# A table of steps for each batch's projections, and rope's products in another PSUM bank, in a decoder layer on one core

## The chip, the cores and the metric

The kernel runs on one core of a Trainium2 chip. Its time is device microseconds of one execution; several executions are timed, and their median is compared. One further execution is recorded by the hardware profiler, and the rows shown here come from it.

## What is computed

A decoder layer on x of shape (4, 512, 128): four batches (0 to 3) of 512 rows. Cut to what matters:

```python
x = x + attn(layernorm(x))      # 16 heads of 8; causal
    q = xn @ W_q                                    # (512, 128)
    lat = layernorm(xn @ W_dkv) * gamma + beta      # (512, 32)
    k, v = lat @ W_uk, lat @ W_uv                   # (512, 128) each
    q, k = rope(q), rope(k)
    softmax(q k^T / sqrt(8), causal) v, then @ W_o
x = x + cross_attn(layernorm(x), ctx)   # 8 heads of 64, 32 context rows
x = x + fp4_ffn(layernorm(x))           # blockwise FP4 of activations and weights, silu(gate) * up
```

Rope on one side (0 is q, 1 is k): the product times cos, plus the product with its halves exchanged times sin.

## The kernel before

**Slots and steps.** The attention of a batch is cut into four groups of four heads. One group is one slot, so batch b fills slots 4b to 4b+3, sixteen slots in all (0 to 15), and every slot has ten steps (0 to 9). Each engine walks the same loop over slots n and steps u, and at each step it issues what the tables and the functions of the kernel give it for that step. The order on each engine is therefore written out by hand; engines meet only by semaphores.

**What a slot does.** TensorE multiplies q and k of the next group for its row maxima (`max_pair`, L1081, into three banks `mxp`, two units to a pair), and VectorE adds the mask and reduces them (`max_unit`, L832, 12 units to a slot). `PAIR_STEPS` and `MAX_STEPS` say at which step: pairs stand at steps 0, 2, 3, 4 and, for the group after, at 7 and 8. At step 6 VectorE writes the maxima as bfloat16 (L842, L844), at step 7 TensorE turns them (`max_rows`, L1090), ScalarE copies them (`nrows`), and SyncE places them with a DMA into `qs`. TensorE's `score_unit` (L1105) at steps 0, 1, 3, 5, 6, 8 feeds ScalarE's exponentials (L633, `exp_unit`), GpSimd masks them (L446) and TensorE multiplies them by the values (L1116). From slot 5 on the rows behind attention go through stages a to d of ten steps each, one tile of 128 rows entering per slot: output projection, cross-attention, FP4 feed-forward. Slots 5, 6 and 7 have one, two and three of them, later ones four. They use the banks `misc[0]` (stages a and b) and `misc[1]` (stages c and d).

**Projections ahead.** While batch b is in attention, batch b+1 is projected (`project`, called as `project(b + 1, g, u)` with g the slot within the batch). One table, `WHEN`, gives each part (slot in the batch, step): layer norm's statistics, `xn`, its transpose `xnT` (L995), the latent product `lat` (L1001), its norm `latn` (L748) and transpose `latT` (L1008, L573), and for each side the product (`cos0`, `cos1`, L1015, 128x512 in float32), the multiplication by cos on VectorE (L779, under the same entry), ScalarE's two copies of 64 rows that exchange halves (`swap`, L543), the multiplication by sin on VectorE (`sin`, L786), then on GpSimd and ScalarE the sum (L286) and its split in three bfloat16 parts (`high`, `rest` L292, `mid`, `low` L298). SyncE stores the parts in DRAM (L344) and loads them in stacked form into `qs` and `ks` (L359); the first max pairs of a batch wait for that at step 7 of the slot 4b+2 that goes before it. `values_in` (L1022) makes the batch's v at slot 4b+1, step 0, from `latT`.

Rope's products stand in `banks[MX_BANK]`, the first of the three `mxp` banks. TensorE's `claim` makes whoever writes a bank wait for the last reader of what it held, so the max pair that follows in this bank waits for the swap.

`set_up` (parts 8 to 10, L1059 and L1063) transposes the feed-forward weights in slot 1. SyncE's own loop is a fixed order of stores, loads and places per slot; at slot 4b+1 it places the maxima of slot 4b+2, then stores and loads the next batch's parts.

Of the kernel before, what the change touches and what calls it, by code (L numbers as in the profile page):

```python
# [84 lines left out]
def decoder_layer(nc, x, ctx_768, L0_attn_W_q, L0_attn_W_dkv, L0_attn_W_uk, L0_attn_W_uv, L0_attn_W_o,  # L85
# [8 lines left out]
    with ctx:  # L94
# [322 lines left out]
        def _(pool):  # L417
# [110 lines left out]
            for n in range(NSLOT + 5):  # L528
                b, g_ = n // NG, n % NG
                for u in range(10):  # L530
# [10 lines left out]
        def _(act):  # L541
# [19 lines left out]
            def project(b, g, u):  # L561
                if (g, u) == WHEN["xnT"]:
                    act.wait_ge(s["xnT_mm"], b + 1)
                    copy(xnT[:, :], misc[0][:, :]).then_inc(s["xnT_d"], 1)
# [710 lines left out]
```

## Time and profile before

| | |
|---|---|
| median of 3 runs | 421.15 us (420.87 to 424.14) |
| profiled execution, its own time | 423.29 us |
| its span, first to last instruction | 421.6 us |
| mean granted TensorE clock | 0.784 |
| TensorE busy | 298.0 us, 71% |
| VectorE busy | 299.5 us, 71% |
| ScalarE busy | 177.5 us, 42% |
| GpSimd busy | 192.8 us, 46% |

The profiled execution lies 2.1 us over the median. The first exponential of slot n marks where the slot begins. These marks stand at 47.5 us for slot 0, 99.6 for slot 3, 111.8 for slot 4, 166.2 for slot 7, 182.2 for slot 8, 249.4 for slot 11 and 320.9 for slot 15. Before 47.5 us lie the loads, batch 0's projections and the set-up of weights; behind slot 15 the rows of the last batch are finished.

### The profile page before, as it was taken

How to read it: one execution, taken by the hardware profiler on the slowest of the kernel's cores; microseconds unless marked ns; L12 is line 12 of the kernel's file. 1: busy time of each engine (PE TensorE's matmuls, PEld its weight loads, DVE VectorE, ACT ScalarE, POOL GpSimd, SP SyncE). 2: the span in 40 equal slices, each digit the busy share in tenths (PEclk: the TensorE clock that was granted, in tenths of full speed). 3: DMA queues.
4: the chain of work that ended last, by engine and by line, in shares of the span. 5: the costliest groups of instructions: out<-in, count | busy, mean ns of one | idle time of the engine just before them, and what ended most of it. 6: DMA issues, size and time to landing. Idle time of an engine off the chain costs nothing.

```text
span 421.6 us, 6515 instructions
## 1 busy us (share of the span) xinstructions
PE 298.0 (71%) x1790; PEld 144.2 (34%) x1790; DVE 299.5 (71%) x1137; ACT 177.5 (42%) x327; POOL 192.8 (46%) x374
## 2 busy tenths in 40 slices
PE   1684678757877768868785979787797664848553
PEld 1272332212234123334432434334243323536332
DVE  5467656446647576898879787899977536677882
ACT  5351355543546354445454435355545412322111
POOL 4214207322306363363757553545545535563653
PEclk9998555756768686889888588899979968665696
DMA  8069000260300052004002600040000000000000
GB/s 214 27 198 178 1 0 4 75 151 0 78 0 1 24 174 32 1 0 83 2 8 75 158 1 8 2 83 7 3 6 3 7 0 8 7 0 9 1 12 19
DMA packets 20835, 17.50 MB, mean 42 GB/s; under 512 B 1920, under 2 KB 20224, under 8 KB 20800
## 3 DMA queue, kind: packets, MB, share of 16 engines
q1 hardware_dynamic: 20272, 16.50, 16.0%
q10 hardware_dynamic: 528, 0.59, 0.5%
q8 instruction: 15, 0.25, 0.3%
q14 instruction: 20, 0.16, 0.1%
HBM read 9.62 MB, written 7.34 MB: 40 GB/s over the span
## 4 chain that ended last, share of the span: by engine, by line
PE 39%; DVE 30%; issue 11%; POOL 8%; DMA 6%; ACT 4%; SPq 1%; DVEq 0%; POOLq 0%; ACTq 0%
PE pvp L1116 9%; DVE summed L832 8%; PE mxp L1081 5%; PE st L1105 4%; DMA ks<-parts_dram 3%; PE mxp L1015 3%; PE misc L1195 3%; PE misc L1180 2%; DMA parts_dram<-parts 2%; DVE space L768 2%; POOL space L476 2%; DVE stats L737 2%; PE misc L1177 2%; DVE space L748 2%; DVE space L765 2%
## 5 line engine op out<-in xcount | busy, mean ns | idle before, releaser
L832 DVE CUSTOM_DVE_ANT_0 summed<-mxp,causal 128x512 bf16<-128x512 f32 (+3 forms) x256 | 114.0, 486 | 19.8 <-PE mxp L1081 19.3
L633 ACT ACTIVATE probs<-st 128x1024 f32<-128x1024 f32 (+1 forms) x96 | 84.6, 881 | 85.4 <-PE st L1105 85.1
L1081 PE MATMUL mxp<-ks,qs 48*128 48x512 bf16 (+3 forms) x256 | 40.8, 357 | 49.1 <-DVE rmax L832 37.9
L1116 PE MATMUL pvp<-probs,va 128*32 128x128 f32 (+3 forms) x512 | 60.4, 558 | 5.1 <-POOL probs L446 5.1
L446 POOL TENSOR_SCALAR_AFFINE_SELECT probs<-probs 128x256 f32<-128x256 f32 x128 | 48.0, 411 | 23.0 <-ACT probs L633 23.0
L543 ACT ACTIVATE space<-misc 128x128 f32<-128x128 f32 (+3 forms) x78 | 24.2, 327 | 48.5 <-PE misc L1136 18.2
L1105 PE MATMUL st<-qs,ks 50*128 50x512 bf16 (+3 forms) x256 | 41.4, 363 | 3.5 <-ACT probs L633 2.2
L1081 PEld LDWEIGHTS mxp<-ks,qs 48*128 48x128 bf16 x256 | 11.9, 98 | 69.4 <-DVE rmax L832 42.5
L476 POOL TENSOR_TENSOR space<-space 128x128 f32<-128x128 f32 (+2 forms) x33 | 24.8, 752 | 23.6 <-DVE space L771 23.6
L463 POOL TENSOR_TENSOR space<-space,xrden 128x256 f32<-128x256 f32 x16 | 9.8, 615 | 40.9 <-DVE xrden L889 40.9
L488 POOL TENSOR_TENSOR space<-space,reciph 128x352 f32<-128x352 f32 x16 | 12.6, 785 | 32.3 <-DVE reciph L759 32.3
L1105 PEld LDWEIGHTS st<-qs,ks 50*128 50x128 bf16 x256 | 10.9, 101 | 45.2 <-issue 27.3
L439 POOL TENSOR_TENSOR rstd<-var,halfneg 128x1 f32<-128x1 f32 (+1 forms) x36 | 23.0, 640 | 3.0
L437 POOL TENSOR_SCALAR var<-mv 128x1 f32<-128x1 f32 (+1 forms) x36 | 9.1, 253 | 27.7 <-DVE mv L741 26.0
L832 DVE DVE_READ_ACCUMULATOR2_ANT rmax<- 128x1 f32 x256 | 21.3, 83 | 0.0
L1116 PEld LDWEIGHTS pvp<-probs,va 128*32 128x32 f32 x512 | 11.8, 121 | 26.8 <-issue 18.5
L765 DVE TENSOR_SCALAR space<-space 128x128 int32<-128x128 int32 (+2 forms) x33 | 12.2, 369 | 9.1 <-POOL space L470 4.5
L1195 PE MATMUL misc<-wdT,space 128*128 128x128 f32 (+1 forms) x72 | 15.8, 377 | 2.3 <-ACT space L543 2.3
L779 DVE TENSOR_TENSOR turned<-mxp,cos 128x512 f32<-128x512 f32 x8 | 5.5, 692 | 16.1 <-PE mxp L1015 16.1
L1195 PEld LDWEIGHTS misc<-wdT,space 128*128 128x128 f32 (+1 forms) x72 | 13.5, 273 | 9.0 <-ACT space L543 7.6
L771 DVE SCALAR_TENSOR_TENSOR space<-space 128x128 f32<-128x128 f32 (+2 forms) x33 | 15.4, 465 | 1.1
L437 POOL TENSOR_SCALAR varl<-mvl 128x4 f32<-128x4 f32 x4 | 0.9, 230 | 29.5 <-DVE mvl L741 29.5
(196 smaller groups left out, 593.9 us busy)
## 6 DMA issues: line engine op xcount, KB each, us to landing
parts_dram<-parts SPq DMA_DIRECT2D x8, 384.0 KB, 2.6
qs<-parts_dram SPq DMA_DIRECT2D x16, 192.0 KB, 3.8
ks<-parts_dram SPq DMA_DIRECT2D x16, 192.0 KB, 4.4
parts_dram<-parts SPq DMA_DIRECT2D x8, 256.0 KB, 2.9
xin<-in_x SPq DMA_DIRECT2D x4, 256.0 KB, 8.2
parts_dram<-parts SPq DMA_DIRECT2D x8, 128.0 KB, 2.9
out<-outr SPq DMA_DIRECT2D x16, 64.0 KB, 1.6
qs<-nrows SPq DMA_DIRECT2D x32, 4.0 KB
```

The source lines that it names most:

```text
L439: g.tensor_tensor(rstd[:, sl], var[:, sl], halfneg[:, sl], ALU.pow).then_inc(s["rstd" + name], 1)
L446: last = g.affine_select(out=m, in_=m, compare_op=ALU.is_ge, fill=0.0, base=0, pattern=[[0, 2], [1, P]], channel_multiplier=-1)
L476: g.tensor_tensor(norm, norm, expo, ALU.subtract).then_inc(s[round_name], 1)
L543: return nc.scalar.activation(dst, src, ACT.Copy, scale=scale)
L633: nc.scalar.activation(probs[n % 2][:, 2 * pair:2 * pair + 2, 512 * k:512 * k + w], st2[:, :].rearrange("p (h q) -> p h q", h=2)[:, :, 0:w ...
L765: v.tensor_scalar(expo.bitcast(i32), norm.bitcast(i32), 0x7F800000, None, ALU.bitwise_and)\
L771: v.scalar_tensor_tensor(norm, norm, BIT_DOWN, expo, ALU.mult, ALU.add).then_inc(s[sum_name], 1)
L832: last = v.tensor_tensor_reduce(out=summed[:, m % 2, e * w:(e + 1) * w], in0=mxp[m % 3][:, e * w:(e + 1) * w], in1=causal[:, S - w:S], sca ...
L1081: last = mm(units[r][:, e * w:(e + 1) * w], qs[rows, c, i * P:(i + 1) * P], ks[rows, c, 0:w], start=True, stop=True)
L1105: last = mm(stp[r][:, at:at + S - P * j], ks[rows, c, j * P:(j + 1) * P], qs[rows, c, j * P:S], start=True, stop=True)
L1116: last = mm(pvp[32 * i:32 * i + 32, j * P:S], va[:, j, GH * (n % NG) + i, :], probs[n % 2][:, i, OFF[j]:OFF[j] + S - P * j], start=(j == 0 ...
L1195: last = mm(m[:, 0:DM], dqhT[0:w, k % R, c * P:(c + 1) * P], wdT[0:w, c, :], start=(c == 0), stop=(c == 2))
```

## The change

`WHEN` becomes a table for each batch (batch 0 shares batch 1's). The entry `turn` is new: VectorE's multiplication by cos gets a step of its own behind TensorE's product, where before both had the step `cos`. `swap` and `sin` follow it. In all batches the latent's statistics and norm come earlier. Batches 2 and 3 have entries with slot -1: their projections begin in the last slot of the batch before the previous one, that is at slots 3 and 7 in place of 4 and 8. The last entry, `low1`, moves from slot 4b+2 step 0 (b the batch that is in attention: slots 2, 6, 10) to slot 1 step 8 for batch 1, slot 4 step 7 for batch 2 and slot 9 step 5 for batch 3. The products go to `ROPE_BANK = 1`, which is `misc[1]`. `latT` becomes a pair of buffers, since batch 2's is written before batch 1's values are made. The three parts of `set_up` move from slot 1 to slot 2. SyncE's order is untouched.

```diff
+ROPE_BANK = 1
...
-WHEN = {"stats": (0, 0), "rstd": (0, 0), "xn": (0, 2), "xnT": (0, 3), "lat": (0, 4), "lat_stats": (0, 8),
...
-        "cos0": (0, 5), "swap0": (0, 6), "sin0": (0, 7), "cos1": (1, 5), "swap1": (1, 6), "sin1": (1, 7),
...
+           "cos0": (0, 5), "turn0": (0, 7), "swap0": (0, 8), "sin0": (0, 9), "sum0": (1, 0), "high0": (1, 1),
...
-SET_UP = [(1, 1), (1, 4), (1, 8)]
+SET_UP = [(2, 1), (2, 4), (2, 8)]
...
-        latT = sb("latT", [P, S])
+        latT = sb("latT", [P, 2, S])
...
-                    if b < B - 1:
-                        project(b + 1, g_, u)
+                    for ahead in range(1, B):
+                        project(ahead, n - NG * (ahead - 1), u)
...
-                    wait(act, "v_mm", b)
-                    nc.scalar.activation(latT[0:LAT, :], misc[0][0:LAT, :], ACT.Identity, bias=beta[:, :],
+                    wait(act, "v_mm", b - 1)
+                    wait(act, "rope_mm", 2 * b - 2)
+                    nc.scalar.activation(latT[0:LAT, b % 2, :], misc[0][0:LAT, :], ACT.Identity, bias=beta[:, :],
...
-                v.tensor_tensor(turned[:, side, 0, :], banks[MX_BANK][:, :], cos[:, :], ALU.mult)\
+                v.tensor_tensor(turned[:, side, 0, :], banks[ROPE_BANK][:, :], cos[:, :], ALU.mult)\
...
-                    if (g, u) == WHEN[f"cos{side}"]:
+                    if (g, u) == WHEN[b][f"turn{side}"]:
                         turn_cos(b, side)
...
-                    if (g, u) == WHEN[f"cos{side}"]:
-                        m = claim(MX_BANK, "swapped_d", 2 * b + side + 1)
+                    if (g, u) == WHEN[b][f"cos{side}"]:
+                        m = claim(ROPE_BANK, "swapped_d", 2 * b + side + 1)
```

The changed kernel's lines stand 16 or 17 further down, so L779 becomes L796, L786 L803, L832 L849, L1015 L1032, L1081 L1098, L1090 L1107 and L1105 L1122.

VectorE in slot 0, batch 1's first rope side, before (L779 is the multiplication by cos; ISA rows are max units, of which those of 128 columns are the last before the maxima are written):

```order
88 L832 ISA rmax 128x1
89 L779 TENSOR_TENSOR turned<-mxp,cos 128x512
90 L832 ISA summed,rmax<-mxp,causal 128x128
91 L832 ISA rmax 128x1
92 L832 ISA summed,rmax<-mxp,causal 128x128
```

and now, from the writing of the maxima at step 6 on:

```order
97 L859 CAST nparts<-rmax 128x8x2
98 L861 TENSOR_TENSOR nparts<-rmax,nparts 128x8x2
99 L754 BN_STATS statsl<-lat 128x6 x4
100 L758 BN_AGGR mvl<-statsl 128x2 x4
101 L796 TENSOR_TENSOR turned<-misc,cos 128x512
102 L849 ISA summed,rmax<-mxp,causal 128x512
103 L849 ISA rmax 128x1
104 L765 TENSOR_SCALAR latn<-lat,mvl,rstdl 128x32 x4
105 L849 ISA summed,rmax<-mxp,causal 128x512
106 L849 ISA rmax 128x1
107 L803 TENSOR_TENSOR turned<-turned,sin 128x512
```

The multiplication by cos has moved from ahead of the last max units and of the maxima's writing to behind both, and the latent's statistics and norm have come into slot 0.

TensorE at the same place, steps 5 to 8, before:

```order
28 L1105 MATMUL st<-qs,ks 128x512 x2
29 L1015 MATMUL mxp<-xnT,wq 128x512
30 L1105 MATMUL st<-qs,ks 128x384 x2
31 L1105 MATMUL st<-qs,ks 128x128 x2
32 L1090 MATMUL mxp<-identb,nparts 8x128 x4
33 L1081 MATMUL mxp<-ks,qs 128x512 x2
34 L1105 MATMUL st<-qs,ks 128x256 x2
35 L1081 MATMUL mxp<-ks,qs 128x512 x2
36 L1105 MATMUL st<-qs,ks 128x512 x2
```

and now:

```order
28 L1122 MATMUL st<-qs,ks 128x512 x2
29 L1032 MATMUL misc<-xnT,wq 128x512
30 L1122 MATMUL st<-qs,ks 128x384 x2
31 L1122 MATMUL st<-qs,ks 128x128 x2
32 L1107 MATMUL mxp<-identb,nparts 8x128 x4
33 L1098 MATMUL mxp<-ks,qs 128x512 x2
34 L1122 MATMUL st<-qs,ks 128x256 x2
35 L1098 MATMUL mxp<-ks,qs 128x512 x2
36 L1025 MATMUL misc<-ident,latn 32x128 x4
37 L1122 MATMUL st<-qs,ks 128x512 x2
```

The product L1015 keeps its place and changes its bank from `mxp` to `misc`. The transpose of the latent (L1025) now stands in slot 0, after two max pairs.

TensorE with batch 3's first side, before (slot 8, steps 5 to 7, with stages a to d around it):

```order
228 L1015 MATMUL mxp<-xnT,wq 128x512
229 L1116 MATMUL pvp<-probs,va 32x512 x4
230 L1105 MATMUL st<-qs,ks 128x384 x2
231 L1105 MATMUL st<-qs,ks 128x128 x2
232 L1180 MATMUL misc<-wguT,space 128x352
233 L1090 MATMUL mxp<-identb,nparts 8x128 x4
234 L1164 MATMUL misc<-vwo,space 128x128 x2
235 L1081 MATMUL mxp<-ks,qs 128x512 x2
```

and now (slot 7, steps 6 and 7):

```order
199 L1197 MATMUL misc<-wguT,space 128x352
200 L1107 MATMUL mxp<-identb,nparts 8x128 x4
201 L1181 MATMUL misc<-vwo,space 128x128 x2
202 L1032 MATMUL misc<-xnT,wq 128x512
203 L1098 MATMUL mxp<-ks,qs 128x512 x2
204 L1133 MATMUL pvp<-probs,va 32x384 x4
```

The product has moved from two steps ahead of the next max pair (L1081) to right in front of it, behind the up product (L1197) that uses the same bank `misc[1]`.

## Rows read from the trace of the kernel before

**Rows 1.** The page's busy times: us, share of the span, instructions.

```profile
PE 298.0 (71%) x1790; PEld 144.2 (34%) x1790; DVE 299.5 (71%) x1137; ACT 177.5 (42%) x327; POOL 192.8 (46%) x374
```

**Rows 2.** Busy time by stretch: slots 0-2, 3, 4-6, 7, 8-10, 12, 13.

```profile
core 0: us, PE busy (x) PEld busy (x) DVE busy (x) ACT busy (x) POOL busy (x), PEclk, DMA share, GB/s
47.50:99.60 52.10, 37.48 (x207) 12.61 (x207) 30.08 (x136) 25.92 (x39) 18.41 (x34) 0.57 0.18 47
99.60:111.80 12.20, 9.87 (x74) 2.88 (x72) 7.86 (x38) 6.26 (x10) 2.41 (x7) 0.71 0.04 10
111.80:166.20 54.40, 41.64 (x262) 15.56 (x260) 35.67 (x156) 27.01 (x44) 23.11 (x46) 0.75 0.23 57
166.20:182.20 16.00, 12.67 (x87) 5.24 (x87) 13.33 (x54) 8.07 (x15) 6.64 (x15) 0.89 0.01 2
182.20:249.40 67.20, 52.84 (x322) 25.65 (x322) 56.37 (x218) 32.31 (x62) 38.19 (x71) 0.82 0.21 51
268.20:286.30 18.10, 14.32 (x100) 7.03 (x101) 16.05 (x64) 8.52 (x17) 9.26 (x20) 0.91 0.25 49
286.30:303.60 17.30, 13.38 (x106) 6.53 (x105) 16.21 (x64) 8.96 (x18) 9.26 (x20) 1.00 0.02 6
```

**Rows 3.** Groups by line: busy us, mean ns | idle before them, what ended it.

```profile
L1081 PE MATMUL mxp<-ks,qs 48*128 48x512 bf16 (+3 forms) x256 | 40.8, 357 | 49.1 <-DVE rmax L832 37.9 <-ACT turned L543 7.6 <-DMA ks<-parts_dram 3.6
L779 DVE TENSOR_TENSOR turned<-mxp,cos 128x512 f32<-128x512 f32 x8 | 5.5, 692 | 16.1 <-PE mxp L1015 16.1
L786 DVE TENSOR_TENSOR turned<-turned,sin 128x512 f32<-128x512 f32 x8 | 5.5, 683 | 9.1 <-ACT turned L543 9.1
L768 DVE TENSOR_SCALAR space<-space 128x128 f32<-128x128 f32 (+2 forms) x33 | 11.8, 358 | 1.1
```

**Rows 4.** Timeline of slot 0: start us, us; in brackets idle before, and releaser.

```profile
56.11 2.08 PE L1015 MATMUL mxp<-xnT,wq 128*128 128x512 f32 x2
58.23 0.69 DVE L779 TENSOR_TENSOR turned<-mxp,cos 128x512 f32<-128x512 f32 x1 [3.42 <-PE mxp L1015]
60.23 0.59 PE L1090 MATMUL mxp<-identb,nparts 128*8 128x128 bf16 x4 [1.50 <-DVE nparts L844]
61.04 0.69 DVE L786 TENSOR_TENSOR turned<-turned,sin 128x512 f32<-128x512 f32 x1 [0.87 <-ACT turned L543]
61.27 0.61 PE L1081 MATMUL mxp<-ks,qs 48*128 48x512 bf16 x2 [0.45 <-ACT turned L543]
```

**Rows 5.** Timeline of slots 1 and 2.

```profile
78.43 0.39 PE L1081 MATMUL mxp<-ks,qs 48*128 48x512 bf16 x2 [2.02 <-ACT turned L543]
...
85.00 1.16 POOL L298 TENSOR_TENSOR parts<-turned,parts 128x512 bf16<-128x512 f32 x1 [0.39 <-ACT parts L543]
...
90.27 0.79 SPq L359 DMA_DIRECT2D ks<-parts_dram  x2
...
94.76 0.61 PE L1081 MATMUL mxp<-ks,qs 48*128 48x512 bf16 x2 [2.90 <-DMA ks<-parts_dram]
```

**Rows 6.** Timeline of slots 4 and 5.

```profile
125.70 0.39 PE L1081 MATMUL mxp<-ks,qs 48*128 48x512 bf16 x2 [2.02 <-ACT turned L543]
...
137.79 2.07 PE L1015 MATMUL mxp<-latT,wuk 128*128 128x512 f32 x2 [1.21 <-DVE rmax L832]
...
144.01 0.41 PE L1081 MATMUL mxp<-ks,qs 48*128 48x512 bf16 x2 [1.72 <-ACT turned L543]
```

**Rows 7.** Timeline of slots 8 to 10.

```profile
194.68 1.02 PE L1015 MATMUL mxp<-xnT,wq 128*128 128x512 f32 x2
...
198.11 1.19 ACT L543 ACTIVATE turned<-mxp 64x512 f32<-64x512 f32 x2
...
224.87 1.29 POOL L286 TENSOR_TENSOR turned<-turned 128x512 f32<-128x512 f32 x1
...
225.07 1.29 DVE L768 TENSOR_SCALAR space<-space 128x352 f32<-128x352 f32 x1
...
229.59 1.14 DVE L765 TENSOR_SCALAR space<-space 128x128 int32<-128x128 int32 x1
```

More of the change, by code:

```diff
@@ L431, in _ @@
                             pattern=[[-1, P]], channel_multiplier=1)
-            g.memset(latT[:, :], 0.0).then_inc(s["consts_ready"], 1)
+            g.memset(latT[:, :, :], 0.0).then_inc(s["consts_ready"], 1)
             def rstd_of(mv, var, rstd, name, sl, n):
@@ L699, in _ @@
             for name in ("xnT", "lat", "swap0", "latT", "high0", "swap1", "mid0"):
-                project(0, *WHEN[name])
+                project(0, *WHEN[0][name])
             set_up(0)
             for name in ("high1", "mid1"):
-                project(0, *WHEN[name])
+                project(0, *WHEN[0][name])
             act.wait_ge(s["cross_ready"], 1)
@@ L719, in _ @@
                         stages[stage](k, step)
-                    if b < B - 1:
-                        project(b + 1, g, u)
+                    for ahead in range(1, B):
+                        project(ahead, n - NG * (ahead - 1), u)
                     if 0 < b < B and (g, u) == VALUES_IN:
@@ L802, in project @@
                 for side in range(2):
-                    if (g, u) == WHEN[f"cos{side}"]:
+                    if (g, u) == WHEN[b][f"turn{side}"]:
                         turn_cos(b, side)
-                    if (g, u) == WHEN[f"sin{side}"]:
+                    if (g, u) == WHEN[b][f"sin{side}"]:
                         turn_sin(b, side)
@@ L943, in _ @@
             sorted_weights()
-            for name in ("lat_stats", "cos0", "latn", "sin0"):
-                project(0, *WHEN[name])
+            for name in ("lat_stats", "turn0", "latn", "sin0"):
+                project(0, *WHEN[0][name])
             rope_sum(dve, v, 0, 0)
-            project(0, *WHEN["cos1"])
+            project(0, *WHEN[0]["turn1"])
             part_rest(dve, v, 0, 0)
-            project(0, *WHEN["sin1"])
+            project(0, *WHEN[0]["sin1"])
             rope_sum(dve, v, 0, 1)
@@ L969, in _ @@
                         stages[stage](k, step)
-                    if b < B - 1:
-                        project(b + 1, g, u)
+                    for ahead in range(1, B):
+                        project(ahead, n - NG * (ahead - 1), u)
                     for ahead, m in MAX_STEPS[u]:
@@ L1003, in project @@
                     last.then_inc(s["lat_mm"], 1)
-                if (g, u) == WHEN["latT"]:
+                if (g, u) == WHEN[b]["latT"]:
                     pe.wait_ge(s["latn_d"], b + 1)
@@ L1021, in values_in @@
                 for t in range(NT):
-                    last = mm(m[:, t * P:(t + 1) * P], latT[:, t * P:(t + 1) * P], wuv[:, :], start=True, stop=True)
+                    last = mm(m[:, t * P:(t + 1) * P], latT[:, b % 2, t * P:(t + 1) * P], wuv[:, :], start=True, stop=True)
                 last.then_inc(s["v_mm"], 1)
@@ L1223, in _ @@
                         stages[stage](k, step)
-                    if b < B - 1:
-                        project(b + 1, g, u)
+                    for ahead in range(1, B):
+                        project(ahead, n - NG * (ahead - 1), u)
                     if 0 < b < B and (g, u) == VALUES_IN:
```

73 lines of the change are left out of this document (40 added, 33 removed), and 13 rows, old and new, of the table WHEN.

## The prediction, made before the changed kernel had run

> **What bounds the kernel now.** I read the busy times first: TensorE and VectorE share the lead at 71% each, so neither is full over the whole span [rows 1]. Then the busy times by stretch, since 71% is a mean over stretches with different limits [rows 2]. The reader is to see three things there. In slots 12 and 13, with four row stages and no projection, VectorE is busy 16.05 of 18.1 us and 16.21 of 17.3 us: VectorE is the bound there, with 1.1 to 2.05 us idle per slot. In slot 3, with neither rows nor projection, a slot takes 12.2 us, and TensorE (9.87 us busy at a granted clock of 0.71) is nearer to its limit than VectorE (7.86 us). And slots with a projection are longer by more than its work: slots 8 to 10 take 67.2 us against 3 x 18.1 = 54.3 us for three of slot 12, an excess of 12.9 us, while VectorE's busy time is up by 56.37 - 3 x 16.05 = 8.2 us only. Slots 0 to 2 take 52.1 us with TensorE busy 37.48, slots 4 to 6 take 54.4 with 41.64: 14.6 and 12.8 us in which TensorE stands. So I looked for what it waits for.
>
> The groups name it [rows 3]: 49.1 us of idle time ahead of the max pairs, of which 37.9 is VectorE still reducing (the ordinary pace of a ring of three banks), but 7.6 is ScalarE's swap, which holds the first `mxp` bank, and 3.6 is the load of `ks`. VectorE stands 16.1 us ahead of its eight multiplications by cos and 9.1 us ahead of the eight by sin. The timelines show how these chain. In slot 0 TensorE's rope product runs 2.08 us at half clock, VectorE waits 3.42 us for it with max units queued behind the multiplication, so the maxima are late and TensorE waits 1.50 us for them, then 0.45 us for the swap [rows 4].
>
> **The change part by part.**
>
> *Batch 1 (slots 0 to 2).* With `turn` two steps behind the product, VectorE reduces its last units and writes the maxima while TensorE multiplies; with the other bank the next max pair doesn't wait for the swap. What leaves TensorE's path: 1.50 + 0.45 us in slot 0 [rows 4] and 2.02 us in slot 1 [rows 5], together 3.97 us. The product itself (about 2 us each) stays on TensorE and stays on its path. The load: the last part is made at 85.00 + 1.16 us, the `ks` load is issued at 90.27, and the first max pair of batch 1 waits for it 2.90 us until 94.76 [rows 5]. Now `low1` comes at slot 1 step 8 in place of slot 2 step 0, two steps earlier; but slot 1 holds more of that lead, since the set-up and the latent's norm have left it. Two steps of a 16 us slot are 3.2 us, just over the 2.90 us, and the set-up now in slot 2 pushes the pair back further. The wait goes. Sum so far 6.9 us. What comes back is VectorE's wait for the swap at the step `sin`, which follows `swap` by one step. The nearest row is the 0.87 us of slot 0, where VectorE had come straight from the maxima [rows 4]; twice that is 1.7 us. Bounds: nothing comes back (6.9), or both swaps are waited for in full, 1.19 us each [rows 7], and the load still holds a half (6.9 - 2.4 - 1.45 = 3.1). I take 6.9 - 1.7 = **5.2 us**.
>
> *Batch 2 (slots 3 to 6).* The first side and the latent move into slot 3, the shortest. The waits that leave TensorE: 2.02 and 1.72 us for the swap, and 1.21 us in which the product waited for the `mxp` bank to be read [rows 6], together 4.95 us. The moved work costs the same wherever TensorE is the limit, so I count nothing for a fuller slot 3. Back come two waits at `sin`, 1.7 us. Bounds 4.95 and 4.95 - 2.4 = 2.6 us; I take **3.2 us**.
>
> *Batch 3 (slots 7 to 10).* Here VectorE is the bound, and the question is its idle time and its lengthened operations. Slots 8 to 10 have 67.2 - 56.37 = 10.8 us idle, against 3 x 2.05 = 6.2 us at slot 12's rate and 3.3 us at slot 13's [rows 2]: excess 4.6 to 7.5 us. Two operations also ran long beside GpSimd's rope work: L768 took 1.29 us, started 0.20 us into the 1.29 us sum L286, and an L765 took 1.14 us; the L768 group has a mean of 0.36 [rows 3, 7]. These are about 0.9 and 0.8 us, 1.7 in all. Rope's GpSimd work moves from steps 8, 9 and 0, where the rounding of FP4 stands on VectorE, to steps 1, 3 and 5 of slots 8 and 9. So 6.3 us could go (up to 9.2). Against it: both products now stand at step 7, right in front of the max pair that VectorE wants next. A product costs 1.02 us at full clock [rows 7] and 2.08 at half [rows 4]; two are 2.0 to 4.2 us, of which before VectorE showed 1.27 as idle only on one. I put 2.1 there. The bank is shared with stages c and d: the product must wait for `hid`, which VectorE issues a step earlier with two TensorE operations between, and stage d's transposes at step 1 wait for the swap of step 9. Half a swap each, 2 x 0.6 = 1.2 us. I take 6.3 - 2.1 - 1.2 = **3.0 us**, bounds 9.2 and -0.3 (6.3 less 4.2 and 2.4).
>
> *Edits at nothing.* The zeroing of `latT` doubles, far ahead of slot 0, beside VectorE's first statistics, for which GpSimd and TensorE wait there anyway. In the prologue the first set-up transpose uses the rope bank and now waits for the swap, but the work behind it waits for batch 0's load in any case. ScalarE's added wait for `rope_mm` names a product two batches old. SyncE's order is the same: it stores batch 2's and 3's parts only after the maxima of slots 6 and 10 are placed, so parts that are ready earlier gain nothing more than the end of the load wait. If the cover in the prologue were gone it would cost half a swap, 0.6 us.
>
> **Sum.** 5.2 + 3.2 + 3.0 = 11.4 us. The profiled execution took 423.3 us by its own time (span 421.6), so it would take 411.9; the median of the runs is 421.15, from which I predict **409.8 us**, 2.7% less. Slots 11 to 15 and the end behind them shift as they are: every slot hangs on the one before through both engines.
>
> **A rule of the Trainium skill on GpSimd's moved work.** The two long operations ran beside GpSimd instructions that read the same memory [rows 7]. The page "SBUF — State Buffer", section "Who interferes with whom", says that VectorE in its two-port modes, or with two SBUF inputs against a reading GpSimd instruction, shares a port pair under an exclusive lock, so that the second to issue blocks for the first's whole length. The trace agrees as far as it goes: VectorE's operation ended with GpSimd's.
>
> **The rivals.**
>
> *The waits only change their name.* TensorE still has two products of 2 us per batch at half clock, in slots where its clock is granted at 0.57 to 0.75 of full [rows 2]. If the max pairs come as late as now, VectorE's waits go from L779 to L832, and what goes is the load's 2.90 us. Against: the 1.50 and 2.02 us are TensorE's own waits, not VectorE's. Time 421.15 - 2.9 = 418.3. Chance 0.14.
>
> *GpSimd's sums hold VectorE six times.* Batch 3's three operations of each side last 1.16 to 1.29 us, and two of six met a VectorE operation that could be held. In the new places next to the multiplication by sin and the norms, all six could, at 0.9 us: 5.4 us in place of 1.7. Then batch 3 gives 3.0 - 3.7 = -0.7 us and the time is 413.5. This is what the lock of that page would do at worst. For it speaks that the multiplication by sin reads two SBUF tensors; against it, that steps 1 to 5 hold mostly reads of PSUM. Chance 0.12.
>
> *Slower: bank 1 and step 7 in the VectorE-bound slots.* Each product at step 7 holds back the max pair by 2.08 us, and each swap at step 9 holds back stage d's transposes, and with them the down product and the bank for stage c, by 1.19 us: 2 x (2.08 + 1.19) = 6.5 us. In batches 1 and 2 the gains then shrink to the load's 2.9 us. Time 421.15 + 6.5 - 2.9 = 424.8. It decides once these handovers cost more than the other batches gain. For it: slots 7 and 8 are the ones without slack. Against: the clock is granted at 0.82 to 0.89 there, so a product is nearer 1.02 us. Chance 0.07.
>
> *More than counted.* TensorE's granted clock is 0.57 in slots 0 to 2, where it stands most, and 1.00 in slot 13, where it hardly does [rows 2]. With fewer waits more of the matmuls run at 2.4 GHz. Taking the upper bounds, 6.9 + 4.95 + 9.2 = 21 us, gives 400; half way between that and the forecast is 405. Chance 0.15 for 401 to 405.
>
> The forecast itself, 405 to 415, has 0.52.
>
> **How the numbers follow.** A measurement of this kernel tells about 1%, or 4.2 us, from no change. Below 416.9 us lie the forecast, the better case and the six holds: 0.79, less some of their edges, 0.78. Within 1%: the renamed waits and a part of the slower rival, 0.16. Over 425.4: 0.06. The range from 402 to 418 leaves out most of the slower rival, half of the renamed waits and the edge of the best case, 2 in 10.
>
> **What would show each step.** In slots 0, 1, 4 and 5, L796 (cos) is preceded by little idle time, under 1 us, and no L1098 waits for ScalarE's swap. Slot 2 loses the wait of L1098 for the `ks` load. L803 (sin) waits 0.5 to 1.2 us. Slots 0 to 2 together take some 47 us, slots 3 to 6 some 63.5, slots 7 to 10 some 80 (83.2 now). No rounding operation (L782, L785) lasts over 1 us beside GpSimd's rope sums. I am wrong if TensorE's waits for `rmax` in slots 7 to 9 grow by what VectorE's waits for L1032 lose, or if the second set-up and latent work simply move the stall from slot 1 to slot 0.

## The result, and the profile after

The changed kernel takes 407.72 us (median of 4 runs, 405.24 to 410.85), the kernel before 422.13 us beside it (4 runs, 420.87 to 424.14). The recorded ratio is 0.972, with a 95% interval of 0.966 to 0.978; the ratio of the two medians is 0.966, at the lower end of it. The forecast was 409.8 us, a ratio of 0.973, so 11.4 us less where the medians show 14.4. Later runs of the same kernel had a median of 404.82 us. The profiled execution took 405.5 us by its own time, span 403.8 us, at a granted clock of 0.804 in place of 0.784. It lies 2.2 us under its median, and the one of the kernel before lies over its own and counts among that kernel's slower runs, so the 17.8 us between the two spans overstate the gain.

Lines have moved by 16 or 17: cos is L796, sin L803, `max_unit` L849, the product L1032, `max_pair` L1098, `max_rows` L1107, the value product L1133, the swap and ScalarE's other copies L559. The busy times of the changed kernel's page, and three of its groups by line:

```profile
PE 288.0 (71%) x1790; PEld 140.9 (35%) x1790; DVE 299.5 (74%) x1137; ACT 176.8 (44%) x327; POOL 193.7 (48%) x374
...
L849 DVE CUSTOM_DVE_ANT_0 summed<-mxp,causal 128x512 bf16<-128x512 f32 (+3 forms) x256 | 113.9, 486 | 23.6 <-PE mxp L1098 23.2
...
L1098 PE MATMUL mxp<-ks,qs 48*128 48x512 bf16 (+3 forms) x256 | 40.0, 349 | 45.1 <-DVE rmax L849 40.9 <-DMA ks<-parts_dram 3.9
L1133 PE MATMUL pvp<-probs,va 128*32 128x128 f32 (+3 forms) x512 | 55.2, 512 | 5.1 <-POOL probs L462 5.1
```

VectorE's busy time has not moved (299.5 us before and after). TensorE's has: the same 1790 matmuls took 298.0 us [rows 1] and take 288.0. So the span's 17.8 us are 10.0 us of shorter matmuls and 7.8 us less idle time (123.6 to 115.8). Of the 10.0 us, 6.2 lie in slots 0 to 10; 3.8 lie ahead of slot 0 and from slot 11 on, where the matmuls are the same in number (155 and 687) and the lengths differ by under 2 us. The value product, which the change does not touch, shows it; its line of before:

```profile
L1116 PE MATMUL pvp<-probs,va 128*32 128x128 f32 (+3 forms) x512 | 60.4, 558 | 5.1 <-POOL probs L446 5.1
```

Its 512 matmuls took 60.4 us, 558 ns each, and now take 55.2 us, 512 ns each. Of the swap's 7.6 us ahead of the max pairs [rows 3] nothing is left; the load of `ks` still holds them 3.9 us, of which 2.15 lie ahead of slot 0 (0.55 there before).

Busy times by stretch: slots 0-2, 3, 4-6, 7, 8-10, 12 and 13, against [rows 2]:

```profile
47.60:92.70 45.10, 35.19 (x207) 12.12 (x207) 31.52 (x143) 25.56 (x38) 18.92 (x34) 0.62 0.21 54
92.70:109.30 16.60, 14.61 (x88) 5.96 (x88) 11.59 (x53) 8.93 (x14) 5.07 (x9) 0.69 0.03 10
109.30:150.40 41.10, 31.12 (x242) 12.02 (x242) 29.69 (x132) 24.39 (x39) 19.64 (x41) 0.88 0.29 75
150.40:174.70 24.30, 19.04 (x103) 8.61 (x103) 18.40 (x80) 10.17 (x20) 11.22 (x23) 0.70 0.00 1
174.70:233.30 58.60, 48.33 (x308) 23.10 (x308) 52.13 (x195) 29.57 (x57) 34.38 (x65) 0.80 0.23 59
251.70:270.50 18.80, 15.08 (x100) 7.51 (x101) 16.24 (x64) 8.44 (x17) 9.26 (x20) 0.82 0.22 47
270.50:287.80 17.30, 13.38 (x106) 6.54 (x105) 16.21 (x64) 9.07 (x18) 9.25 (x20) 1.00 0.02 6
```

Slots 0 to 2 went from 52.1 to 45.1 us, slots 3 to 6 from 66.6 to 57.7, slots 7 to 10 only from 83.2 to 82.9. Slots 12 and 13, without a projection, are as they were but for 0.7 us in slot 12, at a clock of 0.82 in place of 0.91; from slot 11 on the kernel is 1.8 us shorter. In slots 3 to 6 TensorE's busy time went from 9.87 + 41.64 = 51.5 us to 14.61 + 31.12 = 45.7 us, its idle time only from 15.1 to 12.0.

Slots 7 to 10 in one stretch, before and now:

```profile
166.20:249.40 83.20, 65.51 (x409) 30.90 (x409) 69.70 (x271) 40.39 (x76) 44.83 (x86) 0.84 0.17 42
150.40:233.30 82.90, 67.37 (x411) 31.70 (x411) 70.53 (x274) 39.74 (x75) 45.60 (x88) 0.77 0.16 42
```

VectorE's idle time fell from 13.5 to 12.4 us (in slot 7 it rose from 2.7 to 5.9, in slots 8 to 10 it fell from 10.8 to 6.5), and its busy time rose from 69.7 to 70.5.

The timeline of slots 0 to 2 of the changed kernel, against [rows 4, 5]:

```profile
56.22 2.08 PE L1032 MATMUL misc<-xnT,wq 128*128 128x512 f32 x2
58.33 0.69 DVE L796 TENSOR_TENSOR turned<-misc,cos 128x512 f32<-128x512 f32 x1 [0.29 <-PE misc L1032]
58.76 0.59 PE L1107 MATMUL mxp<-identb,nparts 128*8 128x128 bf16 x4
59.28 0.61 PE L1098 MATMUL mxp<-ks,qs 48*128 48x512 bf16 x2
62.38 0.70 DVE L803 TENSOR_TENSOR turned<-turned,sin 128x512 f32<-128x512 f32 x1
...
75.64 1.16 POOL L308 TENSOR_TENSOR turned<-turned,parts 128x512 f32<-128x512 f32 x1 [2.14 <-ACT parts L559]
...
77.91 1.15 POOL L314 TENSOR_TENSOR parts<-turned,parts 128x512 bf16<-128x512 f32 x1 [1.12 <-ACT parts L559]
...
83.16 0.79 SPq L375 DMA_DIRECT2D ks<-parts_dram  x2
...
87.69 0.39 PE L1098 MATMUL mxp<-ks,qs 48*128 48x512 bf16 x2 [1.78 <-DMA ks<-parts_dram]
```

VectorE waits 0.29 us ahead of cos in place of 3.42; neither the transposes of the maxima nor the max pair behind them waits, and nothing waits for the swap at sin. In slot 2 the load holds the max pair 1.78 us (2.90 before). The last part is ready 7.1 us sooner (79.06 against 86.16 us), and the load is issued 4.1 us behind it as before; but without its wait the pair would come 6.0 us sooner too (85.91 against 91.86), so the lead grew by 1.1 us only. In the chain of the parts GpSimd waited 2.14 and 1.12 us for ScalarE's splits.

Slot 7, now with batch 3's first steps in it, takes 24.3 us where it took 16.0:

```profile
151.35 0.86 DVE L754 BATCH_NORM_STATS2 stats<-xin 128x6 f32<-128x128 f32 x4
...
154.63 0.44 PE L1153 MATMUL misc<-ident,att 128*128 128x128 f32 x1 [2.17 <-DVE space L899]
...
157.63 1.54 PE L1194 MATMUL misc<-wguT,space 128*128 128x352 f32 x2
...
165.67 1.52 PE L1197 MATMUL misc<-wguT,space 128*128 128x352 f32 x2
...
167.23 0.52 DVE L935 SCALAR_TENSOR_TENSOR space<-space,misc 128x352 f32<-128x352 f32 x1 [3.56 <-PE misc L1197]
```

The wait of this place before:

```profile
169.32 0.30 PE L1136 MATMUL misc<-ident,att 128*128 128x128 f32 x1 [1.07 <-DVE space L882]
```

Batch 3's statistics (L754) stand on VectorE ahead of the cross-attention rows (L899), for which TensorE waits 2.17 us, 1.07 before. From 153.4 us on the clock is granted at half for 13.7 us, the gate and up products take 1.5 us each, and VectorE, the bound from here on, stands 3.56 us for the second.

### The profile page after: what moved, and what is told of

The parts are those of the page before. It is cut to its first block, busy times and chain, and to the rows that moved or that the text cites. A ratio compares the mean times of both kernels' runs of the same rounds, so it can differ in the third digit from the quotient of the medians.

```text
span 403.8 us, 6515 instructions
## 1 busy us (share of the span) xinstructions
PE 288.0 (71%) x1790; PEld 140.9 (35%) x1790; DVE 299.5 (74%) x1137; ACT 176.8 (44%) x327; POOL 193.7 (48%) x374
## 4 chain that ended last, share of the span: by engine, by line
PE 36%; DVE 34%; issue 12%; POOL 6%; DMA 5%; ACT 5%; SPq 1%; DVEq 0%; POOLq 0%; ACTq 0%
DVE summed L849 9%; PE pvp L1133 6%; PE mxp L1098 4%; PE st L1122 4%; PE misc L1212 3%; PE misc L1032 2%; PE misc L1197 2%; PE pvp L1144 2%; DVE stats L754 2%; DVE space L765 2%; DMA ks<-parts_dram 2%; PE misc L1018 2%; DVE space L785 2%; POOL space L492 2%; DVE space L782 2%
## 5 line engine op out<-in xcount | busy, mean ns | idle before, releaser
L849 DVE CUSTOM_DVE_ANT_0 summed<-mxp,causal 128x512 bf16<-128x512 f32 (+3 forms) x256 | 113.9, 486 | 23.6 <-PE mxp L1098 23.2
L1098 PE MATMUL mxp<-ks,qs 48*128 48x512 bf16 (+3 forms) x256 | 40.0, 349 | 45.1 <-DVE rmax L849 40.9
L1133 PE MATMUL pvp<-probs,va 128*32 128x128 f32 (+3 forms) x512 | 55.2, 512 | 5.1 <-POOL probs L462 5.1
L462 POOL TENSOR_SCALAR_AFFINE_SELECT probs<-probs 128x256 f32<-128x256 f32 x128 | 49.0, 418 | 19.3 <-ACT probs L650 19.3
L559 ACT ACTIVATE space<-misc 128x128 f32<-128x128 f32 (+3 forms) x78 | 24.2, 327 | 48.2 <-PE misc L1153 19.3
L1122 PE MATMUL st<-qs,ks 50*128 50x512 bf16 (+3 forms) x256 | 40.1, 353 | 4.2 <-ACT probs L650 1.8
L1098 PEld LDWEIGHTS mxp<-ks,qs 48*128 48x128 bf16 x256 | 12.0, 97 | 68.6 <-DVE rmax L849 48.2
L1122 PEld LDWEIGHTS st<-qs,ks 50*128 50x128 bf16 x256 | 10.8, 100 | 43.4 <-issue 21.9
L849 DVE DVE_READ_ACCUMULATOR2_ANT rmax<- 128x1 f32 x256 | 21.2, 83 | 0.0
L1133 PEld LDWEIGHTS pvp<-probs,va 128*32 128x32 f32 x512 | 11.1, 115 | 21.4 <-issue 13.2
L782 DVE TENSOR_SCALAR space<-space 128x128 int32<-128x128 int32 (+2 forms) x33 | 11.4, 347 | 7.7 <-POOL space L486 3.1
L559 ACT ACTIVATE nrows<-mxp 8x512 bf16<-8x512 bf16 x16 | 9.3, 580 | 13.5 <-PE mxp L1107 13.4
L896 DVE TENSOR_REDUCE xmax<-misc 128x8 f32<-128x256 f32 x12 | 5.0, 421 | 11.2 <-PE misc L1169 11.1
```

Of the source, the lines that this page charges most:

```text
L462: last = g.affine_select(out=m, in_=m, compare_op=ALU.is_ge, fill=0.0, base=0, pattern=[[0, 2], [1, P]], channel_multiplier=-1)
L559: return nc.scalar.activation(dst, src, ACT.Copy, scale=scale)
L782: v.tensor_scalar(expo.bitcast(i32), norm.bitcast(i32), 0x7F800000, None, ALU.bitwise_and)\
L849: last = v.tensor_tensor_reduce(out=summed[:, m % 2, e * w:(e + 1) * w], in0=mxp[m % 3][:, e * w:(e + 1) * w], in1=causal[:, S - w:S], sca ...
L1098: last = mm(units[r][:, e * w:(e + 1) * w], qs[rows, c, i * P:(i + 1) * P], ks[rows, c, 0:w], start=True, stop=True)
L1122: last = mm(stp[r][:, at:at + S - P * j], ks[rows, c, j * P:(j + 1) * P], qs[rows, c, j * P:S], start=True, stop=True)
```

## Experiments

All the kernels below are the changed one with one part put back or moved (two batches in one case), but for the bank alone, which is the kernel before with one edit. For a part "wholly undone" the old steps, where `turn` stands with the product, go with the old bank, by a list `ROPE_BANK[b]` of one bank per batch. They were measured in three groups of four, each beside the kernel before: rows 3 to 6 of the table, then rows 7 to 10, both on one chip, and rows 11 to 14 on another. Ratios are taken to the kernel before of the same group. In the first group the recorded ratios of rows 3 to 5 correspond to some 421 us for it and that of row 6 to some 419 us, so these four are best compared by their medians. The changed kernel itself has 0.972 in one group and 0.962 in the other, which is the size of difference that these ratios can't tell. Lengths are from mark to mark in each profile; "half" is the time at the granted clock 0.5.

| kernel | median us | ratio, 95% interval | slots 0-2 | 3-6 | 7-10 | 11 to end | half in the four |
|---|---|---|---|---|---|---|---|
| before | 422.13 | | 52.1 | 66.6 | 83.2 | 172.2 | 45, 34, 27, 66 |
| changed | 407.72 | 0.972 (0.966 to 0.978) | 45.1 | 57.7 | 82.9 | 170.4 | 34, 21, 38, 56 |
| bank only, old steps | 427.92 | 1.015 (1.007 to 1.023) | 50.1 | 67.3 | 89.0 | 170.6 | 40, 42, 38, 59 |
| cos joined again | 409.38 | 0.971 (0.963 to 0.979) | 48.7 | 59.2 | 82.7 | 170.8 | 42, 22, 34, 59 |
| batch 3: old steps | 409.84 | 0.970 (0.961 to 0.979) | 44.2 | 59.4 | 86.1 | 170.2 | 38, 27, 31, 52 |
| 2 and 3: old steps | 417.88 | 0.997 (0.992 to 1.002) | 44.1 | 61.7 | 90.6 | 171.6 | 26, 24, 41, 73 |
| changed, again | 404.82 | 0.962 (0.953 to 0.970) | 44.6 | 57.5 | 82.8 | 170.6 | 34, 21, 34, 56 |
| batch 3 wholly undone | 407.47 | 0.970 (0.962 to 0.978) | 44.5 | 57.6 | 80.1 | 169.3 | 26, 17, 17, 52 |
| batch 1 wholly undone | 413.84 | 0.985 (0.978 to 0.992) | 52.5 | 58.6 | 82.5 | 172.0 | 45, 27, 34, 64 |
| batch 3 sooner | 404.70 | 0.964 (0.957 to 0.971) | 43.2 | 60.8 | 76.4 | 173.2 | 29, 14, 21, 66 |
| batch 2 wholly undone | 416.97 | 0.988 (0.981 to 0.995) | 44.8 | 64.9 | 82.5 | 177.1 | 34, 34, 34, 86 |
| set-up back in slot 1 | 405.43 | 0.965 (0.958 to 0.973) | 44.3 | 57.6 | 82.8 | 170.8 | 37, 21, 34, 59 |
| batch 3 sooner, old bank | 413.39 | 0.981 (0.973 to 0.988) | 43.2 | 67.7 | 79.8 | 173.1 | 29, 35, 30, 66 |
| batch 3's first part sooner | 402.37 | 0.956 (0.950 to 0.961) | 45.3 | 62.1 | 74.0 | 171.4 | 34, 24, 17, 59 |

**The bank alone.** The kernel before, with its products in `misc[1]`:

```diff
+ROPE_BANK = 1
-    m = claim(MX_BANK, "swapped_d", 2 * b + side + 1)
+    m = claim(ROPE_BANK, "swapped_d", 2 * b + side + 1)
```

> The kernel before with one edit: rope's products use misc[1]; table, joint step for product and cos, and set-up as before. If the waits of the max pairs for ScalarE's swap (7.6 us over six) were each on the path, this alone gives 3 to 5 us, ratio to before 0.988 to 0.993. If VectorE's wait for the product (L779, 12.9 us in slots 0 to 10) is what sets the pace, the max pairs then wait for VectorE in place of the swap and the ratio is 0.997 to 1.003.

Neither reading held. It is slower than the kernel before by 1.5%: slots 0 to 2 gain 2.0 us and slots 7 to 10 grow by 5.8 us. No max pair waits for the swap any more, but in slots 8 and 9 the up product does, 2.33 us each time. In slot 8 of this kernel (the up product is L1181, its reader L919):

```profile
199.25 0.86 PE L1181 MATMUL misc<-wguT,space 128*128 128x352 f32 x2 [2.33 <-ACT turned L544]
...
200.15 0.52 DVE L919 SCALAR_TENSOR_TENSOR space<-space,misc 128x352 f32<-128x352 f32 x1 [2.57 <-PE misc L1181]
```

The feed-forward's up product needs the bank that waits for rope's swap. The bank is no gain by itself. The converse, batch 1's new steps in the old bank, was not tried: the max pair of step 7 would need the bank before the swap of step 8.

**Cos joined again.** The new tables, but each `turn` in the step of its product:

```diff
-"cos0": (0, 5), "turn0": (0, 7), "swap0": (0, 8)
+"cos0": (0, 5), "turn0": (0, 5), "swap0": (0, 8)
```

> The changed kernel with the multiplication by cos back at the step of the product in all batches; new tables, new bank, set-up in slot 2 kept. If the separate step is what the prediction took it for (1.5 us per side in batches 1 and 2), this is 3 to 5 us slower than the changed kernel, ratio to before 0.979 to 0.984. If TensorE's own work sets the pace, VectorE's wait costs nothing and the ratio stays at 0.972.

Slots 0 to 2 take 48.7 us. In slot 0 the two old waits stand again, in the new bank:

```profile
58.43 0.69 DVE L796 TENSOR_TENSOR turned<-misc,cos 128x512 f32<-128x512 f32 x1 [3.42 <-PE misc L1032]
...
60.44 0.59 PE L1107 MATMUL mxp<-identb,nparts 128*8 128x128 bf16 x4 [1.50 <-DVE nparts L861]
```

So it is `turn`, not the bank, that takes away the 1.50 us. It is worth some 4 us of profile in slots 0 to 2 and 1.5 in slots 3 to 6. The median is 1.7 us over the changed kernel's, less than the 3 to 5 us of the expectation, and with 0.8% on either side the runs don't resolve it.

**Batch 3, and batches 2 and 3, at the old steps**, in the new bank:

```diff
-WHEN[3] = {"stats": (-1, 0), ... "cos0": (-1, 7), "turn0": (-1, 8), ...
+WHEN[3] = {"stats": (0, 0), ... "cos0": (0, 5), "turn0": (0, 5), ...
```

> The changed kernel with batch 3's steps from the old table (starting in slot 8, product and cos in one step), in the new bank. In the profile slots 7 to 10 took 83.0 us after and 83.2 before. If batch 3's new steps are worth the 3.0 us of the prediction and the profile only shows TensorE at half clock for 13.7 us of slot 7, this is 2.5 to 4 us slower than the changed kernel, ratio 0.979 to 0.982. If the new steps of batch 3 give nothing, the ratio stays at 0.970 to 0.974.

> As the one before, with batch 2's steps from the old table too; batch 1's new steps, the bank and the set-up in slot 2 stay. The profile shows 8.9 us won in slots 3 to 6 where 3.2 were predicted. If batch 2's own steps win that, this is 6 to 9 us slower than the kernel with only batch 3 old, ratio 0.987 to 0.993. If most of it came from batch 1's part and from the clock that TensorE is granted after it, it is 2 to 3 us slower, ratio 0.975 to 0.980.

With batch 3 at old steps slots 7 to 10 take 86.1 us (82.8 to 82.9 changed), and the waits of the first experiment are here twice:

```profile
184.03 1.02 PE L1197 MATMUL misc<-wguT,space 128*128 128x352 f32 x2 [2.34 <-ACT turned L559]
185.08 0.52 DVE L935 SCALAR_TENSOR_TENSOR space<-space,misc 128x352 f32<-128x352 f32 x1 [2.73 <-PE misc L1197]
...
210.59 0.86 PE L1197 MATMUL misc<-wguT,space 128*128 128x352 f32 x2 [2.33 <-ACT turned L559]
211.48 0.52 DVE L935 SCALAR_TENSOR_TENSOR space<-space,misc 128x352 f32<-128x352 f32 x1 [2.57 <-PE misc L1197]
```

The median, 409.84 us, is 2.1 us over the changed kernel's 407.72 and 5.0 over its 404.82, and the ratio, 0.970, is between its two: the runs don't resolve these 3.2 us.

With batch 2 at old steps as well the median is 8.0 us higher, 417.88 us, as the first reading had it, and nearly the whole gain is gone (ratio 0.997). But the profile puts only 2.3 us of it in slots 3 to 6 (61.7 against 59.4 us) and 4.4 us in slots 7 to 10, where the two kernels have the same steps.

**Batch 3 wholly undone, batch 1 wholly undone**, beside the changed kernel once more:

```diff
+ROPE_BANK = (1, 1, 1, 4)     # batch 3; for batch 1: (1, 4, 1, 1)
```

> The changed kernel itself, as the anchor for the three others on this chip. Ratio to before 0.966 to 0.978.

> The changed kernel with all of batch 3 undone: old steps and the old bank mxp, batches 0 to 2 in misc[1]. With old steps in misc[1] the up product waited twice 2.3 us for the swap and slots 7 to 10 took 86.1 us. If that wait is all that the bank costs, slots 7 to 10 take 81 to 83.5 us, and the kernel is 0 to 3 us faster than the changed one. If VectorE's wait for product and swap is worth as much as the bank, slots 7 to 10 take 86 us again and it is 2 to 4 us slower.

> The changed kernel with all of batch 1 undone: old steps, old bank for batch 1, set-up in slot 1. If batch 1's part is worth what the profile shows (7 us in slots 0 to 2, of which the prediction had 5.2), slots 0 to 2 take 51 to 53 us and the kernel is 5 to 8 us slower than the changed one, ratio 0.984 to 0.991. If a lower clock in the slots behind gives or takes the difference, the slots 3 to 6 move by over 2 us too.

Without batch 1's part (its set-up is back in slot 1 too) slots 0 to 2 take 52.5 us against 44.6, and the median is 9.0 us over the changed kernel's. Without batch 3's part slots 7 to 10 take 80.1 us against 82.8, with 17 us at half clock against 34. Its six runs fall in two groups, 400.58 (the profiled one) and 403.17 us, and 407.15 to 408.73 us; the changed kernel's lie between 399.42 and 408.44. So its median of 407.47, 2.7 us over, says little, and even the sign of batch 3's part is open: it brings nothing that can be measured.

**Batch 2 wholly undone**, by its old table and `ROPE_BANK = (1, 1, 4, 1)`.

> The changed kernel with batch 2's steps and bank as before; batches 1 and 3 stay changed. Theory (batch 2's part is mis-sized in my sum: waits of the old steps and the half clock that follows them): slots 3 to 6 take 63 to 67 us against 57.7, the time is 5 to 9 us over the changed kernel's 405 to 408, 411 to 416. Rival (my term of 3.2 us was right, and the rest of the 8.9 us came from batch 1's parts through the clock): slots 3 to 6 take 60 to 62 us, time 408 to 411.

Slots 3 to 6 of this kernel, and the two max pairs that wait for the swap again:

```profile
92.00:156.90 64.90, 50.66 (x330) 18.50 (x330) 42.40 (x190) 33.27 (x52) 24.35 (x49) 0.74 0.19 50
```

```profile
118.08 0.39 PE L1098 MATMUL mxp<-ks,qs 48*128 48x512 bf16 x2 [2.19 <-ACT turned L559]
...
136.98 0.39 PE L1098 MATMUL mxp<-ks,qs 48*128 48x512 bf16 x2 [1.82 <-ACT turned L559]
```

Against the changed kernel's 57.7 us that is 7.2 us more: TensorE's idle time is 14.2 us against 12.0, its 330 matmuls take 50.7 us against 45.7. The median is 11.5 us over that of the set-up run of its group, so a part of 3.2 us is out, as it was by the 8.0 us above. In the two profiles (spans 416.4 and 403.4 us) 7.3 us of the 13.0 are this stretch, and 6.3 lie from slot 11 on, where the kernels are the same and the clock was at half for 86 us in place of 59. How much of the median's 11.5 us is such a stretch and how much the part can't be told.

How the part divides is less sure. In the kernel with batches 2 and 3 at old steps in the new bank, TensorE's idle time in slots 3 to 6 was 14.8 us, near the 14.2 here, but its matmuls took 46.9 us, only 1.1 over the changed kernel's, with 24 us at half clock and not 34. Between the two stand the swap's two waits of this kernel, batch 3's steps, and chance; no run separates them.

**The set-up back in slot 1**, at steps 0, 4 and 8.

```diff
-SET_UP = [(2, 1), (2, 4), (2, 8)]
+SET_UP = [(1, 0), (1, 4), (1, 8)]
```

> The changed kernel with the last three set-up steps back in slot 1 (steps 0, 4 and 8; step 1 would stand between batch 1's product and its swap on one bank). Theory (moving them out of slot 1 brings a part of the gain, because batch 1's parts are then ready before the max pairs that want them): slots 0 to 2 take 1.5 to 3 us more than 44.6 to 45.1, with the wait for ks in slot 2 back over 2.5 us. Rival (they fill idle time wherever they stand): slots 0 to 2 within 1 us of 45, the same time within 1%.

Slots 0 to 2 take 44.3 us and the pair waits 0.37 us for `ks`. With the set-up in slot 2 and the same slots 0 to 2, this wait was 1.78 us in the changed kernel's profile and anything from none to 2.81 us in the others', so the 0.37 us is no effect of its own. The rival holds: the lengths show no cost or gain of either slot.

**Batch 3 sooner**: all its steps in slots 6 and 7, in the new bank, in the old one, and only its first part (to the latent's transpose).

```diff
-WHEN[3] = {"stats": (-1, 0), ... "lat_stats": (-1, 7), "latn": (0, 0), "latT": (0, 3), "cos0": (-1, 7), ...
+WHEN[3] = {"stats": (-2, 0), ... "lat_stats": (-2, 6), "latn": (-2, 8), "latT": (-2, 9), "cos0": (-1, 7), ...
```

> The changed kernel with batch 3 one slot sooner still, in slots 6 and 7, on batch 2's pattern of steps (second side one step earlier, to leave misc[1] before stage c enters it). If what batch 3 lacks is slack on VectorE and a free misc[1], slots 6 to 10 take 92 to 95 us (98.8 in the changed kernel) and it is 4 to 7 us faster, ratio 0.956 to 0.963. If slots 6 and 7 only grow by what 8 to 10 lose, the ratio stays at 0.972.

> The changed kernel with batch 3 in slots 6 and 7 and batch 3's products in the first mxp bank. In batch 3 bank 1 costs where stages c and d use it too (slots 7 on), the bank of the max pairs costs where they are on the path. Theory (the shared bank is a cost in slot 7 only at old steps): like the sooner version with bank 1, slots 3 to 10 together 136 to 139 us, 403 to 407 us. Rival (bank 1 holds the row stages in the new steps as well): slots 7 to 10 take 2 us or more less than that version's 76.4, 400 to 403 us.

> The changed kernel with batch 3's statistics, transposes and latent product in slot 6 in place of slot 7; its rope steps stay in slots 7 to 9. Theory (slot 7 takes 24.3 us because batch 3's statistics stand on VectorE in front of the row stage, TensorE stands 2.2 us and then runs at half clock): slot 7 takes 19 to 21 us, slot 6 gains 1.5 to 2 us, slots 3 to 10 together 138 us against 140.7, 402 to 406 us. Rival (the work costs its length wherever it stands): slots 3 to 10 within 1 us of 140.7, 405 to 408 us.

Slots 3 to 10 take 137.2 us with everything sooner, 147.5 with that in the old bank, and 136.1 with the first part alone, against 140.6 of the changed kernel. With everything sooner the median is that of the changed kernel all the same (404.70 against 404.82 us), so the expected 4 to 7 us did not come. The old bank costs 1.7% of time here by the two ratios, of two groups, and both theories on it had it wrong: TensorE waits 3.9 us for two swaps and is at half clock for 34.5 us of slots 3 to 6, against 13.7 us with everything sooner in the new bank. The last kernel has the lowest median of the study: 402.37 us (401.59 to 403.56), against 405.43 us (404.11 to 410.12) of the set-up run in its group, which is otherwise the changed kernel. No run of the one reaches into the range of the other, though their intervals of the ratio overlap, at 0.958 to 0.961. The profile says where the gain lies. Its slots 6, 7 and 8 to 10:

```profile
135.50:155.50 20.00, 16.39 (x102) 7.68 (x100) 14.70 (x70) 8.86 (x15) 7.65 (x18) 0.74 0.41 110
155.50:172.80 17.30, 13.53 (x89) 5.51 (x89) 15.20 (x58) 9.30 (x17) 8.27 (x18) 0.90 0.00 1
172.80:229.60 56.80, 45.39 (x304) 22.15 (x304) 51.62 (x192) 29.06 (x57) 34.77 (x66) 0.88 0.24 61
```

```profile
158.69 0.30 PE L1153 MATMUL misc<-ident,att 128*128 128x128 f32 x1 [1.07 <-DVE space L899]
...
166.10 0.52 DVE L935 SCALAR_TENSOR_TENSOR space<-space,misc 128x352 f32<-128x352 f32 x1 [0.45 <-PE misc L1197]
```

Slot 7 is 17.3 us, VectorE is busy for 15.2 of them, and the clock in it is 0.90; the wait of 2.17 us is 1.07 us again, and that of 3.56 us is 0.45. Slot 6 pays 4.2 us for the work it took; over slots 3 to 6 VectorE's busy time is 4.4 us more and its idle time the same, 16.5 against 16.4 us. Slot 7 lost 3.2 us of VectorE's busy time and 3.8 us of its idle time. That the place of this first part as a whole (statistics, norm, transposes and latent product) sets slot 7's length is shown. Which of its instructions does it, and that it does so through the clock, is the reading of these rows, since no run moved one without the other.

## Why the prediction was right, and where its steps were not

The time (409.8 against 407.72 us) is right with wrong terms: 5.2, 3.2 and 3.0 us for the three batches were 7.0, 8.9 and 0.3 in the profile, and 1.8 behind them. That batch 2 gave much more and batch 3 nothing, so that the sum came near, is luck.

**Batch 1: 5.2 us, measured 7.0 (7.9 when undone alone).** The mechanism was as written: waits of 1.50, 0.45 and 2.02 us are gone. TensorE's idle time fell by 4.7 us, from 14.6 to 9.9, near the 5.2 us, but two steps of the sum were wrong and nearly cancel. The load's wait was to go and only fell from 2.90 to 1.78 us: I counted how much sooner the last part comes and left out that the pair comes sooner too. And 1.7 us were to come back at `sin`: ahead of the sin of both of batch 1's sides VectorE doesn't stand at all, since max units fill the time. The other 2.3 us of the 7.0 are shorter matmuls, which no term had. That the set-up's move helps is not borne out.

**Batch 2: 3.2 us, measured 8.9 (7.3 when undone alone).** This is the mis-sized term. As a sum of waits it was near: TensorE's idle time fell by 3.1 us. That too had parts that cancel: the waits of 4.95 us are gone and nothing to speak of came back at `sin` (0.2 us), but TensorE's waits for VectorE's reductions grew from 5.0 to 6.7 us and those of the scores for the placed maxima to 1.5 us. What I left out is the matmuls' own length. I wrote that "the moved work costs the same wherever TensorE is the limit", but its busy time fell by 5.8 us, as the granted clock rose from 0.75 [rows 2] to 0.88 in slots 4 to 6 (in slot 3 it went from 0.71 to 0.69). With batch 2 undone in its old bank 4.9 us of it are back, with batches 2 and 3 at old steps in the new bank only 1.1. So the runs show that the part is larger than 3.2 us, and the changed kernel's profile puts the rest in TensorE's busy time; that the new steps are what keeps the clock up there is argued. The clock was a rival of its own ("more than counted"), with the right mechanism and the wrong place: in slots 0 and 1, at 0.57 before, the clock stayed at half up to 78.3 us although the waits were gone. Its 401 to 405 us hold the later median of 404.82 us, not the first.

**Batch 3: 3.0 us, measured 0.3 (the other way when undone alone: 2.7 us shorter without it).** The sum was 4.6 us of VectorE's idle time and 1.7 us of lengthened operations to win, less 2.1 and 1.2 us. The idle time came out as summed, 1.1 us less against 1.3, and this again by luck. Slots 8 to 10 lost 4.4 us of it; slot 7 gained 3.2, but not at the places that I named. VectorE stands for neither product there any more (2.1 us before, of 1.27 and 0.78; I had read the 1.27 as all), and no row stage waits for the swap. What it waits for is the up product, 3.56 us: batch 3's first part, with its statistics ahead of the row stage, was none of my counter-terms, and moving that part to slot 6 takes 4.5 us off slots 3 to 10. So slot 7's growth of 8.3 us is 5.1 us of work that left the slots behind it and 3.2 us of standing. The step that failed outright is the 1.7 us. Operations of VectorE that last over 0.1 us more than the median of their kind lost 2.6 us in slots 7 to 10 before and 2.9 us now: they were to go and are other ones.

**The rivals.** *The waits only change their name*: no; VectorE's wait for max pairs grew from 19.3 to 23.2 us, less than the 12.0 us that it lost at cos and the 8.1 us at sin. *GpSimd's sums hold VectorE six times*: no rounding beside them lasts over 1 us, but another operation is held three times, where before all sixteen took 0.174 to 0.176 us. GpSimd's operation and VectorE's cast of the maxima end within 0.03 us of each other:

```profile
72.23 1.26 POOL L302 TENSOR_TENSOR turned<-turned 128x512 f32<-128x512 f32 x1
72.51 1.01 DVE L859 CAST nparts<-rmax 128x16 bf16<-128x16 f32 x1
...
186.72 1.16 POOL L314 TENSOR_TENSOR parts<-turned,parts 128x512 bf16<-128x512 f32 x1
187.05 0.86 DVE L859 CAST nparts<-rmax 128x16 bf16<-128x16 f32 x1
...
206.73 1.15 POOL L314 TENSOR_TENSOR parts<-turned,parts 128x512 bf16<-128x512 f32 x1
207.41 0.50 DVE L859 CAST nparts<-rmax 128x16 bf16<-128x16 f32 x1
```

The second profile of this kernel has the same three, of 1.01, 0.86 and 0.50 us.

This agrees with the Trainium skill, "SBUF — State Buffer", section "Who interferes with whom", which counts casts, where their operands allow it, among the operations that can take the shared port pair, the second to issue being blocked. The two long roundings of before, which the prediction said ended with GpSimd's operation, ended 0.20 and 0.08 us behind it. *Slower by bank 1*: the collision is real, 2.3 us at a time, but at the up product and at the old steps, where two of them, 4.7 us, stand in slots 8 and 9, against the 5.8 us by which the bank alone lengthens slots 7 to 10; at the new steps the changed kernel shows no wait of the up product for the swap.

**The signs.** Held: under 1 us (0.33 at most) ahead of the cos of batches 1 and 2, whose products stand in slots 0, 1, 3 and 4, not in 4 and 5 as the sign says; no max pair waits for the swap; no long rounding. The two signs of being wrong did not show: TensorE's waits for `rmax` in slots 7 to 9 stayed at 6.7 us, and slot 0 fell as well as slot 1 (17.2 to 16.1 us, 18.7 to 15.4). Slots 0 to 2 took 45.1 us (47 named), slots 3 to 6 57.7 (63.5), slots 7 to 10 82.9 (80). Not held: the load's wait, and the waits at sin.

## What to carry to other kernels

Split TensorE's busy time from its idle time before and after: a wait that is removed can pay more in the matmuls behind it than in itself, and a wait that is added can cost more. Before work is moved into a stage, look at what stands in a row there on the engine that others wait for, down to the first operation; a stage that is slack on average may have none at its start. A bank and the steps that use it are one edit: here the new bank with the old steps cost 1.5%, and for batch 3 the sooner steps in the old bank cost 1.7%; batch 1's and batch 2's new steps in the old bank were not tried.

## What the runs showed of the hardware

TensorE's clock fell to half from 153.4 us on, during a stand of 2.17 us, and stayed for 13.7 us; slot 7 had 11 to 15 us at half in all six profiles in which batch 3's statistics stood there, and 3.4 us in the one in which they and the rest of the first part alone had been moved out. It is not the only thing that sets it: with the rope steps moved too, slot 7 had 7.2 us at half in the new bank and 17.1 us in the old one. What half clock costs differs by stretch: with batch 1's part as changed, slots 0 to 2 took 43.2 to 45.3 us with anything from 26 to 38 us at half. From slot 11 on, where every kernel has the same instructions, the length was 169.3 us with 52 us at half and 177.1 us with 86. That spread, larger than several of the effects here, is in single profiles; it is why the verdicts go by the medians and the causes by the named waits.
